# A two-attention, two-MoE-FFN transformer kernel: the shared expert's last 512 tokens moved behind the experts, expert tiles released in four levels, results stored as four plain rows per token

## The reference

```
x = x + attn_a(layernorm(x))     # grouped heads, rotary, causal softmax
x = x + ffn(layernorm(x))        # FFN "f"
x = x + attn_b(layernorm(x))     # differential attention
x = x + ffn(layernorm(x))        # FFN "h", the same weights

def ffn(x):                      # 16 experts of inner width 176, TOPK = 4, shared width 352
    scores  = softmax(x @ Wg.T)
    masked  = scores of the 2 best of 4 groups of experts
    topi    = top_k(masked, 4);  weights = scores at topi
    y = sum over the 4 experts of weights * (silu(x @ W1.T) * (x @ W3.T)) @ W2.T
    z = silu(x @ Ws1.T) * (x @ Ws3.T) @ Ws2.T          # shared expert
    return y + z
```

## Time and profile before

| | |
|---|---|
| median of 3 runs | 1354.8 us (1343.55, 1354.8, 1356.92) |
| the profiled execution | 1349.85 us |
| its span in the trace | 1348.1 us |
| busy share of the span | PE 85%, PEld 46%, DVE 65%, ACT 40%, POOL 51% |
| mean granted PE clock | 0.934 of 2.4 GHz |
| DMA | 169.84 MB, 126 GB/s over the span |

### The profile page before, as it was taken

The page is one execution under the profiler, slowest core; times in us unless marked ns, Lnnn a source line. Parts: engine busy times, 40 slices in busy tenths (PEclk is TensorE's granted clock), DMA queues, the critical chain, the costliest instruction groups (busy, mean ns, idle before and its releaser), DMA issues.

```text
span 1348.1 us, 26055 instructions
## 1 busy us (share of the span) xinstructions
PE 1144.7 (85%) x8706; PEld 614.0 (46%) x8706; DVE 873.5 (65%) x2067; ACT 541.6 (40%) x846; POOL 689.1 (51%) x841
## 2 busy tenths in 40 slices
PE   6888999998899699999288899999779859999990
PEld 2343444342655366566154344444246435665650
DVE  5688899981576145555388899999568523554543
ACT  2124777779431122222032577777844001222210
POOL 4452344544036577767552454545521652787671
PEclk9897999999889799999699899999988978999995
DMA  4424433320825479987754321221062345898868
GB/s 144 144 86 126 122 109 121 106 64 2 287 72 149 150 183 164 158 156 113 192 178 143 108 61 53 62 50 50 3 255 48 113 129 144 168 159 161 153 91 262
DMA packets 145875, 169.84 MB, mean 126 GB/s; under 512 B 20240, under 2 KB 130768, under 8 KB 145232
## 3 DMA queue, kind: packets, MB, share of 16 engines
q1 hardware_dynamic: 115856, 128.79, 32.7%
q0 software_dynamic: 29184, 38.36, 16.7%
q10 hardware_dynamic: 704, 1.02, 0.2%
HBM read 93.29 MB, written 76.18 MB: 126 GB/s over the span
## 4 chain that ended last, share of the span: by engine, by line
PE 57%; DVE 18%; issue 6%; DMA 6%; ACT 6%; POOL 2%; SPq 2%; another core or an unknown queue 1%; POOLq 0%; ACTq 0%; DVEq 0%
PE pair_ps L1996 11%; PE o_ps L1761 9%; ACT arena L849 4%; DVE nm L1123 4%; PE pair_ps L2029 4%; DMA x_slots<-y_sb,slot_i 3%; DVE bm L1123 3%; PE pair_ps L2032 2%; PE t_ps L1787 2%; PE pair_ps L1711 2%; PE pair_ps L1592 2%; PE pair_ps L1691 2%; PE pair_ps L1716 2%; PE pair_ps L2003 2%; PE pair_ps L1686 2%
## 5 line engine op out<-in xcount | busy, mean ns | idle before, releaser
L849 ACT ACTIVATE arena<-pair_ps 128x1024 f32<-128x1024 f32 x320 | 322.9, 1024 | 130.6 <-PE pair_ps L1686 75.9
L625 POOL TENSOR_SCALAR_AFFINE_SELECT arena<-arena 128x512 f32<-128x512 f32 (+1 forms) x320 | 175.0, 547 | 241.4 <-ACT arena L849 240.9
L1123 DVE TENSOR_REDUCE nm<-pair_ps 128x2 f32<-128x1024 f32 (+1 forms) x192 | 232.6, 1222 | 33.4 <-PE pair_ps L1735 29.5
L687 POOL DMA_INDIRECT x_slots<-y_sb,slot_i x128 | 123.6, 966 | 168.0 <-DVE slot_i L1321 94.0
L1761 PE MATMUL o_ps<-arena 128*9 128x512 f32 (+7 forms) x2048 | 176.8, 440 | 4.2 <-POOL arena L625 4.1
L1996 PE MATMUL pair_ps<-arena 128*128 x512 | 168.6, 471 | 2.5 <-ACT arena L900 2.5
L1123 DVE TENSOR_REDUCE bm<-pair_ps 128x8 f32<-128x1024 f32 x128 | 155.3, 1217 | 4.1 <-PE pair_ps L1735 1.0
L703 POOL DMA_INDIRECT y_h<-xnT,dest x80 | 125.3, 1567 | 58.6 <-DVE xnT L1480 31.4
L703 POOL DMA_INDIRECT y_f<-xnT,dest x80 | 124.6, 1558 | 42.0 <-issue 21.2
L1463 DVE TENSOR_TENSOR arena<-arena,pair_ps 128x128 f32<-128x128 f32 x144 | 41.4, 288 | 116.6 <-ACT arena L905 77.1
L1996 PEld LDWEIGHTS pair_ps<-arena 128*128 128x128 f32 x512 | 93.8, 195 | 43.9 <-issue 6.3
(11 more groups left out here) (275 smaller groups left out, 2012.8 us busy)
## 6 DMA issues: line engine op xcount, KB each, us to landing
arena<-x_slots SPq DMA_DIRECT2D x128, 132.5 KB
arena<-in_w SPq DMA_DIRECT2D x4, 2816.0 KB, 18.9
arena<-q_a SPq DMA_DIRECT2D x64, 96.0 KB
arena<-q_b SPq DMA_DIRECT2D x64, 96.0 KB
y_f<-hw SPq DMA_DIRECT2D x11, 512.0 KB, 2.9
y_h<-hw SPq DMA_DIRECT2D x11, 512.0 KB, 2.9
arena<-in_w SPq DMA_DIRECT2D x2, 2048.0 KB, 17.4
arena<-y_f SPq DMA_DIRECT2D x8, 512.0 KB
```

The lines of the kernel that those rows point to most:

```text
L625: pool.affine_select(p, p, pattern, ALU.is_ge, 0.0, base=0, channel_multiplier=-1)\
L687: pool.indirect_dma_start(x_slots, bass.IndirectOffsetOnAxis(ap=slot_i[:, t, k:k + 1], axis=0), y_sb[:, t, :], None).then_inc(sm(f"scat{n ...
L849: act.activation(p_ring[:, U % RING, :], pair_ps[:, pair_at("T", n, u)].rearrange("p a c -> p (a c)"), ACT.Exp, scale=SCALE).then_inc(sm(" ...
L1123: dve.tensor_reduce(dst, src, X, ALU.max, negate=not 2 <= u < 4).then_inc(sm("t_max_done"), 1)
```

## The change

- `shared_in`, the SiLU, `weigh` and `shared_out` of the last batch (k = 9, 10, 11) move behind the last expert pair, on all engines; their output goes to `s_ps` in place of `t_ps` and `o_ps`. In "f" they lie beside the start of attention b's prologue.
- The order of the tiles knows four levels, 6, 8, 10 and 12 token tiles. SP waits for 24 landed scatters before tile 0, for 32 before tile 8, 40 before 16, 48 before 24, and 64 before 32.
- The three accumulators go. Each (token, choice) has its own row in a DRAM tensor `y_f` or `y_h` of 8192 rows, written by one plain indirect DMA for each tile (72 in place of 80). `x_sb` is no longer stored, the 22 DMAs that cleared the accumulators go, and the rows of `x_slots` carry 268 values in place of 265.
- SP reads all four rows per token back, 8 DMAs of 1 MB with 4 KB per partition and tile; DVE adds them two tiles at a time. The last batch's two wait until the shared expert is done.
- POOL has 40 scatters ahead of the first result, then two after each of the first 12. Every eighth scatter waits for the scatter just before it to land.
- The mixed tiles stand at 35, 39, ... 63.

The core of the diff:

```diff
-MIX = tuple(range(29, NJ, 6))
+MIX = tuple(range(35, 64, 4))
+LEVELS = (6, 8, 10, 12)
+FIRST_X = 40
...
-            for b in range(B - 1):
-                store_x(b)
             sp.wait_ge(sm("padded"), 16 * NE * (1 + past(f, 1)))
-            for parity in range(2):
-                sp.wait_ge(sm(f"scat{parity}"), 16 * (EARLY_T * TOPK // 2 + past(f, NT * TOPK // 2)))
             for j in range(NJ):
-                if j == 4:
-                    store_x(B - 1)
...
+                for t, first in zip(LEVELS + (NT,), (0,) + tuple(TOPK * t - NE for t in LEVELS)):
+                    if j == first:
+                        for parity in range(2):
+                            sp.wait_ge(sm(f"scat{parity}"), 16 * (t * TOPK // 2 + past(f, NT * TOPK // 2)))
                 load(j)
...
+                if b == B - 1:
+                    sp.wait_ge(sm(f + "_hw_used"), 3 * B + 2)
+                for u in (0, 2):
+                    sp.dma_start(back[b][:, u:u + 2], rows[:, b * TB + u:b * TB + u + 2])\
+                        .then_inc(sm(f"load{2 * b + u // 2}"), 16)
...
+                if n > 0 and n % 8 == 0:
+                    pool.wait_ge(sm(f"scat{(n - 1) % 2}"), 16 * ((n + 1) // 2 + past(f, NT * TOPK // 2)))
...
+                pool.indirect_dma_start(y_rows[f], bass.IndirectOffsetOnAxis(ap=dest[:, j:j + 1], axis=0),
+                                        yt[:, j % XR, :], None).then_inc(sm(f"store{j % XR}"), 16)
...
-            for n in range(TH * TOPK, EARLY_T * TOPK + LATE_FIRST):
+            for n in range(TH * TOPK, FIRST_X):
                 scatter(n)
-            late = range(EARLY_T * TOPK + LATE_FIRST, NT * TOPK)
+            late = range(FIRST_X, NT * TOPK)
...
+        def dve_sum(dve, f, q):
...
+            dve.tensor_tensor(part[:, :, 0:2, :], part[:, :, 0:2, :], part[:, :, 2:4, :], ALU.add).then_inc(sm("back_half"), 1)
+            dve.wait_ge(sm("back_half"), done)
+            dve.tensor_tensor(part[:, :, 0, :], part[:, :, 0, :], part[:, :, 1, :], ALU.add).then_inc(sm("back_sum"), 1)
+            dve.wait_ge(sm("back_sum"), done)
+            dve.wait_ge(sm("e_z_free"), TB * (b + 1) + past(f, NT))
+            dve.tensor_tensor(x_sb[:, t:t + 2, :], x_sb[:, t:t + 2, :], part[:, :, 0, :], ALU.add).then_inc(sm(f + "_x"), 2)
...
+            pe.wait_ge(sm("e_y_ev"), NJ + past(f, NJ))
+            shared_in(3 * B - 3)
+            shared_in(3 * B - 2)
+            shared_out(3 * B - 3)
+            shared_in(3 * B - 1)
+            shared_out(3 * B - 2)
+            shared_out(3 * B - 1)
```

More of the change, by code:

```diff
@@ L529, in sp_ffn_back @@
                 sp.wait_ge(sm(f"store{q}"), 16 * (NJ // XR) * (1 + past(f, 1)))
-            sp.wait_ge(sm("store_second"), 16 * MIXED * (1 + past(f, 1)))
+            rows = y_rows[f][0:ROWS * TOPK, :].rearrange("(t p k) e -> p t k e", p=P, k=TOPK)
             for b in range(B):
-                for a, to in ((0, x_sb), (1, back), (2, back2)):
-                    rows = y_acc[f][a][b * T:(b + 1) * T, :].rearrange("(t p) e -> p t e", p=P)
-                    sp.dma_start(to[:, b * TB:(b + 1) * TB, :], rows).then_inc(sm(f"load{2 * b + a % 2}"), 16)
+                if b == B - 1:
[3 more added lines that the diff above has]
+                        .then_inc(sm(f"load{2 * b + u // 2}"), 16)
         @block.sync
@@ L637, in pool_combine @@
             pool.tensor_tensor(osq[:, n % 2], yv, yv, ALU.mult).then_inc(sm("b_sq"), 1)
-        def pool_back(pool):
-            pool.wait_ge(sm("back_sum"), TB)
-            for t in range(TB, NT):
-                if t % TB == 0:
-                    for q in (2 * (t // TB), 2 * (t // TB) + 1):
-                        pool.wait_ge(sm(f"load{q}"), 16 * loads(q))
-                pool.tensor_tensor(back[:, t, :], back[:, t, :], back2[:, t, :], ALU.add).then_inc(sm("back_sum"), 1)
         def pool_out_bias(pool, t):
@@ L896, in act_ffn @@
                 act.activation(sil[0:m, k % 2, :], st_ps[0:m, k % 2, 0:512], ACT.Silu).then_inc(sm("e_sil"), 1)
+            for k in range(3 * (B - 1)):
+                shared_silu(k)
             def pair_in(p):
@@ L916, in act_ffn @@
                     silu(2 * p + 3)
+            for k in range(3 * (B - 1), 3 * B):
+                shared_silu(k)
         @block.scalar
@@ new lines, in dve_back, with z_ps, dve_add_shared @@
+        def dve_back(dve, t):
+            if t % 2 == 0:
+                dve_sum(dve, "f", t // 2)
+                dve.wait_ge(sm("f_x"), t + 2)
+            dve_stats(dve, 2, t)
+        def z_ps(b, u):
+            return (s_ps[:, u // 2] if b == B - 1 else t_ps if u < 2 else o_ps)[:, (u % 2) * E:(u % 2) * E + E]
+        def dve_add_shared(dve, f, b):
+            dve.wait_ge(sm(f + "_hw_used"), 3 * b + 3 + 2)
+            for u in range(TB):
+                t = TB * b + u
+                dve.tensor_tensor(x_sb[:, t, :], x_sb[:, t, :], z_ps(b, u), ALU.add).then_inc(sm("e_z_free"), 1)
@@ L1436, in dve_ffn @@
             assign(0)
-            weigh(0)
+            dve_weigh(dve, f, 0)
             scores(1)
-            weigh(1)
+            dve_weigh(dve, f, 1)
             choose(1)
-            for k in range(2, 3 * B):
-                weigh(k)
+            for k in range(2, 3 * (B - 1)):
+                dve_weigh(dve, f, k)
                 if k % 3 == 0:
-                    add_shared(k // 3 - 1)
+                    dve_add_shared(dve, f, k // 3 - 1)
                 if k == 2:
@@ L1541, in _ @@
             dve_ffn(dve, "h")
-            for t in range(NT):
-                dve_back(dve, "h", t)
+            for q in range(2 * B):
+                if q < 3:
+                    dve_weigh(dve, "h", 3 * (B - 1) + q)
+                dve_sum(dve, "h", q)
+                if q == 2:
+                    dve_add_shared(dve, "h", B - 1)
         def pe_turn(pe, s, b, u):
@@ L1660, in pe_prologue @@
             for b in range(B):
+                if s == "b" and b == 1:
+                    pe.wait_ge(sm("e_z_free"), NT)
                 for k in range(8):
@@ L1909, in counts @@
                     first = max(t + 1, hf * TH)
-                    n = (TH if hf == 0 else NT + 1) - first + (1 if hf == 1 and t < EARLY_T else 0)
+                    n = (TH if hf == 0 else NT + 1) - first + (sum(t < first_t for first_t in LEVELS) if hf == 1 else 0)
                     mm = pe.matmul(s_ps[:, 0, first * NE:(first + n) * NE].rearrange("p (n e) -> p n e", n=n), ones,
@@ L1954, in pe_ffn @@
             shared_in(1)
-            for k in range(3 * B):
+            for k in range(3 * (B - 1)):
                 if k == 1:
```

226 lines of the change are left out of this document (87 added, 139 removed).

## The result

| | changed | before | ratio |
|---|---|---|---|
| median, each of 8 runs | 1365.08 us (1362.52 to 1370.77) | 1353.55 us (1343.55 to 1358.14) | 1.0104, 95% interval 1.0073 to 1.0136 |
| the profiled execution | 1365.39 us | 1349.85 us | |
| its span | 1363.4 us | 1348.1 us | |

The change makes the kernel 1% slower, where 1319 us, about 3% faster, were forecast.

The account below looks back on a forecast made before the run. PE was taken to bound the expert stages, DMA to set their start in "f", and nothing to compute at each FFN's end. From 1349.85 us, -16 in "f" and -15 in "h" gave 1319 us; range 1298 to 1343.

Parts of the forecast that it names:

- Expert start in "f": PE's first expert tile in "f" begins at 436.2 in place of 458.43: -22.2 us.
- clock term: First expert matmuls in "f" run at a better clock after a shorter idle gap: -1 us, bounds 0 and -3.
- "f", POOL: Expert stage of "f": DVE waits slightly for POOL's stores, at 3.8 us per tile: +2 us, +9 at 4.47.
- "h", POOL: Expert stage of "h": POOL finishes its 40 scatters before PE starts, so result 0 goes out at once: 0.
- Expert start in "h": PE's first expert tile in "h" comes at 1108.6 in place of 1124.60: -16.0 us.
- the first rival: PE's 18.12 us wait in the shared expert of "h" goes away, giving 1302 us; chance 0.15.
- End of "f": From the last result of "f" (T), PE starts attention b at T+20.9 in place of T+23.75: -2.8 us.
- prologue: Attention b's prologue after "f": DVE takes over POOL's adds: +8 us, bounds 4 and 12.
- a shared expert that ends after T+17: Sign of a wrong forecast: the shared expert behind the experts, expected near T+16, ends after T+17.
- Tail of "h": From the last result of "h" (T), the span ends at T+35.9 against T+35.2: +1 us.
- POOL as the new bound: First 12 tiles of each FFN: POOL slower, 6.9 us per tile, 35 us lost in each, 1389 us; chance 0.05.
- The other two: Rivals: POOL's results stay at 4.47 us per tile, 1335 us (0.17); start in "f" gains only 2.5, 1339 us (0.10).

Follow-up runs that it names:

- c5: The changed kernel, unaltered, on chip 2: 1320.21 us, ratio 0.9948 to the kernel before.
- e3: The changed kernel without the wait of every eighth scatter, on chip 0: 1298.07 us, ratio 0.9777 to the kernel before.
- e2: The kernel before plus only the wait of every eighth scatter for the preceding one's landing, on chip 0: 1347.15 us, ratio 1.0155.
- e11: The changed kernel with one small POOL memset ahead of each scatter between results, on chip 2: 1324.48 us, ratio 0.9975 to the kernel before.
- e12: The changed kernel with one small POOL memset ahead of each scatter between results, on chip 9: 1327.02 us, ratio 0.9975 to the kernel before.
- e13: The changed kernel without the wait of every eighth scatter, with a small memset ahead of every scatter, on chip 9: 1313.55 us, ratio 0.9868.
- e10: The changed kernel with 52 scatters ahead of the first result in place of 40, on chip 2: 1341.46 us, ratio 1.0090 to the kernel before.
- e9: The changed kernel with shared-expert steps 9 to 11 back in front of the experts, on chip 2: 1327.25 us, ratio 0.9989.

## Why the prediction was wrong

- **Expert start in "f" (-22.2)**: right, -22.3 from the first scatter on. The clock term (-1) was about right too: the first eight first-layer matmuls take 2.63 us in place of 5.05.
- **"f", POOL (+2)**: this step failed, twice over. On the chip of the comparison the stage grew by 32.4 us. On a calm chip it grew by 10.8 (c5, 201.3, against the 190.5 of the first comparison; the unaltered kernel before has no calm trace), of which the rests are 8.2 (e3: 193.1). I had let the rests cancel against `x_sb`'s stores, and had overlooked that they also fall between results. They don't cancel: result 0 was put 65.2 us after the first scatter, and goes out after 69.4, 68.8 in c5 and, without rests, 65.1 in e3. From there to the last scatter c5 takes 49.7 us and e3 44.9. What is left, 2.6 us, is my +2. The other 21.6 us of 32.4 are late starts, for which the sum has no term. The bounds (to +9) came from POOL's pace alone.
- **"h", POOL (0)**: wrong also on a calm chip. I said that POOL has its 40 scatters done before PE starts. With the first tile 38 us sooner after the first scatter that is no longer so (result 0 20.2 us behind PE's first tile in c5): the stage takes 199.2, +10.9. With late starts it is +35.4.
- **Expert start in "h" (-16)**: -38.4 from the first scatter, since the 18.12 us wait went, as in the first rival; without it -20. The rival was right in part: the wait isn't fixed to the code. But late starts came in another place, the stretch that the change made denser. I had weighed a stall without releaser as something that stays or goes, not as something that a denser stream of POOL enlarges.
- **End of "f" (-2.8) and prologue (+8)**: PE starts at T+20.5 (T+20.9 forecast). The prologue costs +13 in place of +8, slightly over its bound of 12: sum +9.7 against +5.2. DVE holds PE for 4.19 us at 690.91. The sign "a shared expert that ends after T+17" came true: its last matmuls end at T+20.7, where I had it done near T+16, and PE goes from them straight to attention b.
- **Tail of "h" (+1)**: +0.4, T+35.6 (T+35.9). Readback issued at T+4.1 (T+3.6), first sum at T+9.2 (T+8.9). The pieces came faster than I said, at 413 GB/s (last number of the row below, of 1340 to 1344 us). It won nothing, because eight sums of 2.64 us, three `weigh` and `add_shared` are then DVE's own bound.

```profile
1340.00:1344.00 4.00, 3.94 (x15) 2.32 (x14) 3.88 (x6) 0.59 (x1) 0.00 (x0) 1.00 1.03 413
```

  By the Trainium skill, DMA: Bandwidth & Descriptors, section iDMA fabric, the rate is 408.7 GB/s, and the trace agrees (408 to 416 from 1336 to 1352); the 3.5 us that I worked out from it didn't come, for DVE's sake.
- **Rivals**: POOL as the new bound (1389, chance 0.05) had the right place, the first tiles of each FFN, and not the right mechanism: POOL kept its 3.8 us per tile, and the others waited, not for it. The other two didn't occur.
- That c5 takes 1320 us is no success of the forecast of 1319: on that chip the kernel before takes 1328, and the gain is 8 us, not 31. Probably the wait of 18.12 us is missing in the kernel before there; no trace of it on a calm chip shows this, but e2's, the same kernel with rests on chip 0, has none.

What stays open: which resource makes PE's signals late, and why chips 4, 10 and that of the first comparison have late starts and 0, 2 and 9 don't, or whether it was the time and not the chip. Whether distance alone (e11, e12, e13), fewer scatters between results (e10) or the shared expert's place (e9) would matter on a disturbed chip wasn't found out, as all came to a calm one. Nor did any run put another kind of DMA in the place of POOL's indirect ones. No version here beats both kernels on both kinds of chip: e3 is best on a calm chip and among the worst on a disturbed one, and there none beat the kernel before.

## What to carry to other kernels

A stall with no releaser that shows on several engines at once is a warning about what another engine does at that time: look at whose signal ended each wait and how late it came, look at what POOL issues, count how long it goes without a pause, and ask whether the change makes such a stretch longer. Price a wait in a stream at every place where that stream passes it, not only where it was meant. And compare on more than one chip before trusting a ratio of 2%: here one kernel stood at 0.978 on one chip and at 1.033 on another.
